# Score matmuls of a 16-head attention: from 128 partitions with masked keys to the head's own 32 partitions

## The reference

```python
q = (x @ Wq + bq).reshape(B, T, H, D).transpose(0, 2, 1, 3)      # B 4, T 1024, H 16, D 8
k = (x @ Wk + bk).reshape(B, T, H, D).transpose(0, 2, 1, 3)
v = (x @ Wv + bv).reshape(B, T, H, D).transpose(0, 2, 1, 3)
scores = jnp.einsum('bhqd,bhkd->bhqk', q, k) * D ** -0.5
scores = scores + slopes[None, :, None, None] * (i - j)          # first attention only
scores = jnp.where(causal, scores, -jnp.inf)                     # first attention only
out = jnp.einsum('bhqk,bhkd->bhqd', softmax(scores), v)
out = out.transpose(0, 2, 1, 3).reshape(B, T, C) @ Wo + bo
```

## Time and profile before

| what | value |
| --- | --- |
| median of 3 runs | 2288.22 us (2284.65 to 2291.63) |
| profiled execution, span | 2287.5 us |
| TensorE matmul busy | 2102.9 us, 92% |
| VectorE busy | 1671.8 us, 73% |
| ScalarE busy | 1373.5 us, 60% |
| POOL busy | 977.3 us, 43% |
| mean granted TensorE clock | 0.959 of full |
| at1 | from about 50 to 740 us |
| at2 | from about 803 to 1720 us |

### The profile page before, as it was taken

How to read it: one execution, slowest core, us unless ns; L and a number is a source line. 1 busy time by engine, 2 the same in 40 slices (tenths; PEclk the granted TensorE clock), 3 DMA queues, 4 the chain that set the end, 5 groups by cost and what they waited for, 6 DMA issues and landing times. The chain is left out here.

```text
span 2287.5 us, 41083 instructions
## 1 busy us (share of the span) xinstructions
PE 2102.9 (92%) x11100; PEld 1223.1 (53%) x11100; DVE 1671.8 (73%) x3157; ACT 1373.5 (60%) x2647; POOL 977.3 (43%) x744
## 2 busy tenths in 40 slices
PE   5899999999999679999999999999993999999996
PEld 4455555555554534555555555555531666666664
DVE  5766667666672787777777777778822899998986
ACT  4266566666666616666666666666672655555654
POOL 3665464553610355333333333342002466565554
PEclk7799999999999679999999999999996999999998
DMA  2000000000000300000000000000001100000000
GB/s 59 1 2 1 3 1 1 2 2 1 1 1 2 110 0 1 2 1 1 2 1 1 2 1 1 1 1 1 1 1 61 51 19 19 2 19 19 19 10 10
DMA packets 27508, 24.96 MB, mean 11 GB/s; under 512 B 2409, under 2 KB 21110, under 8 KB 27282
## 3 DMA queue, kind: packets, MB, share of 16 engines
q1 hardware_dynamic: 26400, 21.91, 3.2%
q10 hardware_dynamic: 882, 0.36, 0.1%
HBM read 13.87 MB, written 6.29 MB: 9 GB/s over the span
## 5 line engine op out<-in xcount | busy, mean ns | idle before, releaser
L466 DVE TENSOR_REDUCE at_mx<-at_a 128x1 f32<-128x512 f32 (+3 forms) x1632 | 1010.8, 675 | 358.7 <-PE at_a L333 249.5
L415 ACT ACTIVATE at_probs<-at_b 128x512 f32<-128x512 f32 (+3 forms) x1792 | 888.6, 558 | 474.0 <-PE at_b L360 292.7
L333 PE MATMUL at_a<-at_km,at_fq 128*128 128x512 f32 (+1 forms) x1632 | 704.8, 439 | 20.4 <-DVE at_mx L466 9.8
L360 PE MATMUL at_b<-at_fqm,at_km 128*128 128x512 f32 (+3 forms) x1792 | 710.8, 404 | 11.4 <-ACT at_probs L415 7.6
L333 PEld LDWEIGHTS at_a<-at_km,at_fq 128*128 128x128 f32 x1632 | 316.3, 194 | 290.0 <-DVE at_mx L466 224.4
L360 PEld LDWEIGHTS at_b<-at_fqm,at_km 128*128 128x128 f32 x1792 | 339.8, 191 | 205.5 <-ACT at_probs L415 120.3
L378 PE MATMUL at_pv<-at_probs,at_vst 128*32 128x512 f32 (+3 forms) x3584 | 437.9, 561 | 1.5 <-ACT at_probs L415 1.5
L556 POOL TENSOR_TENSOR at_hi<-at_u,split_sign 128x512 fp32r<-128x512 f32 x120 | 124.9, 1041 | 441.1 <-ACT at_u L404 306.5
L1172 ACT ACTIVATE t_hid<-t_bank_h,b1t 128x512 f32<-128x512 f32 x256 | 174.3, 689 | 195.9 <-DVE t_hid_lo L1306 113.1
L1306 DVE TENSOR_TENSOR t_hid_lo<-t_hid,t_hid_hi 128x512 fp32r<-128x512 f32 x256 | 225.6, 917 | 15.0 <-ACT t_hid_hi L1179 11.8
L569 POOL TENSOR_TENSOR at_km<-at_fk,head_mask 128x2048 fp32r<-128x2048 f32 x60 | 216.1, 3602 | 11.2 <-POOL at_fk L567 11.0
(11 more groups left out here) (211 smaller groups left out, 2410.3 us busy)
## 6 DMA issues: line engine op xcount, KB each, us to landing
t_raw<-L_ffn_W SPq DMA_DIRECT2D x16, 256.0 KB, 3.1
x_first<-L_attn_x SPq DMA_DIRECT2D x4, 512.0 KB, 7.3
second_x_in<-L_attn_x SPq DMA_DIRECT2D x8, 256.0 KB, 3.1
kept<-second_joined SPq DMA_DIRECT2D x8, 256.0 KB, 2.6
kept_u<-second_normed SPq DMA_DIRECT2D x8, 256.0 KB, 2.0
t_heads_in<-tokens SPq DMA_DIRECT2D x8, 256.0 KB, 2.6
t_u_in<-kept_u SPq DMA_DIRECT2D x8, 256.0 KB, 3.1
t_x_in<-kept SPq DMA_DIRECT2D x8, 256.0 KB, 3.1
```

Source lines behind the costliest of these rows:

```text
L333: mm = pe.matmul(scores, fq[g][:, qt * P:(qt + 1) * P], km[g][:, heads[0]:heads[0] + k, kh * HALF:kh * HALF + w], start=True, stop=not dia ...
L360: mm = pe.matmul(out[:, 0:w], km[g][:, j, kt * P:(kt + 1) * P], fqm[g % 2][:, q0:q0 + w], start=True, stop=not diagonal)
L415: act.activation(probs[(t % 2) * GH + j][:, 0:w], b_bank[n % 3][:, 0:w], ACT.Exp).then_inc(exp_done, 1)
L466: dve.tensor_reduce(mx[:, kh, qt, heads[0]:heads[0] + k], a_bank[n % 3][:, 0:k * w].rearrange("p (k w) -> p k w", k=k), AX.X, ALU.max).the ...
```

## The change

Keys are no longer copied per head. The split writes `fk` for a whole slot, as `fq` is, and `km` with its multiplication goes, on VectorE (first slot) and POOL. Each score matmul takes the 32 partitions of its head from both operands, so that head j lies at row group j. The mask matmuls L337 and L363 still contract 128 partitions. An `a` chunk holds one head, so at1 has 48 chunks in a slot where it had 38; at2 keeps 64. The `b` matmuls and Exps of a step go through the heads in the order 2, 3, 0, 1 (`b_head`). The step counts of the splits' semaphores follow.

```diff
--- before.py
+++ after.py
@@ -65,10 +65,8 @@
...
                     continue
-                per = max(1, HALF // n)
-                per = 4 if per >= 4 else per
-                for j in range(0, GH, per):
-                    self.chunks.append((qt, kh, list(range(j, j + per)), n))
+                for j in range(GH):
+                    self.chunks.append((qt, kh, j, n))
 
@@ -154,6 +152,12 @@
...
 
+def b_head(n):
+
+
+    return (n + 2) % GH
+
+
 class Register:
@@ -217,13 +221,12 @@
...
 
-        km = [sb(f"km{i}", [P, GH, T], F32R) for i in range(4)]
+        fk = [sb(f"fk{i}", [P, T], F32R) for i in range(4)]
         fq = [sb(f"fq{i}", [P, T], F32R) for i in range(4)]
...
         part = sb("part", [P, HALF])
-        fk = sb("fk", [P, HALF])
         probs = [sb(f"probs{i}", [P, HALF]) for i in range(8)]
@@ -317,7 +320,7 @@
...
                     elif what == "a":
-                        qt, kh, heads, w = plan.chunks[n]
+                        qt, kh, j, w = plan.chunks[n]
                         _, g = where(b0, g0, ds)
@@ -325,17 +328,14 @@
...
                         done(pe, a_read, NA, s - back, k)
-                        out = a_bank[n % 3]
+                        scores = a_bank[n % 3][:, 0:w]
                         diagonal = causal and kh * HALF + w == (qt + 1) * P
-
-                        k = len(heads)
-                        scores = out[:, 0:k * w].rearrange("p (k w) -> p k w", k=k)
-                        mm = pe.matmul(scores, fq[g][:, qt * P:(qt + 1) * P],
-                                       km[g][:, heads[0]:heads[0] + k, kh * HALF:kh * HALF + w],
+                        rows = slice(HW * j, HW * (j + 1))
+                        mm = pe.matmul(scores, fq[g][rows, qt * P:(qt + 1) * P],
+                                       fk[g][rows, kh * HALF:kh * HALF + w],
                                        start=True, stop=not diagonal)
                         if diagonal:
-                            mm = pe.matmul(scores[:, :, w - P:w], ident16[:, :],
-                                           causal_mask[:, None, :].broadcast_to([P, k, P]),
+                            mm = pe.matmul(scores[:, w - P:w], ident16[:, :], causal_mask[:, :],
                                            start=False, stop=True)
@@ -347,7 +347,7 @@
...
                         _, g = where(b0, g0, ds)
-                        t, j = n // GH, n % GH
+                        t, j = n // GH, b_head(n)
                         qh, kt = plan.quads[t]
@@ -357,8 +357,9 @@
...
                         out = b_bank[n % 3]
-                        mm = pe.matmul(out[:, 0:w], km[g][:, j, kt * P:(kt + 1) * P],
-                                       fqm[g % 2][:, q0:q0 + w], start=True, stop=not diagonal)
+                        rows = slice(HW * j, HW * (j + 1))
+                        mm = pe.matmul(out[:, 0:w], fk[g][rows, kt * P:(kt + 1) * P],
+                                       fqm[g % 2][rows, q0:q0 + w], start=True, stop=not diagonal)
                         if diagonal:
@@ -405,12 +406,12 @@
...
                     elif what == "b":
-                        t, j = n // GH, n % GH
+                        t, j = n // GH, b_head(n)
                         qh, kt = plan.quads[t]
...
                         done(act, b_made, NB, s, n)
-                        if j == 0:
+                        if n % GH == 0:
                             done(act, pv_done, NQ, s, t - 2)
@@ -436,7 +437,7 @@
...
                         un = u[n % 2]
-                        own = 5 * h if m else 5 * h + 3
+                        own = 4 * h + 2 * (n % 2)
                         done(dve, proj_read, 4, s, n)
@@ -445,26 +446,16 @@
...
                         dve.wait_ge(dve_step, own + 2)
-                        if m == 0:
-                            dve.tensor_tensor(fq[g][:, half], part[:, :], un[:, :],
-                                              ALU.add).then_inc(split_done, 1)
-                        else:
-                            dve.tensor_tensor(fk[:, :], part[:, :], un[:, :], ALU.add).then_inc(dve_step, 1)
-                            dve.wait_ge(dve_step, own + 3)
-                            dve.tensor_tensor(km[g][:, :, half],
-                                              fk[:, None, :].broadcast_to([P, GH, HALF]),
-                                              head_mask[:, :, None].broadcast_to([P, GH, HALF]),
-                                              ALU.mult).then_inc(split_done, 1)
+                        dst = fk if m else fq
+                        dve.tensor_tensor(dst[g][:, half], part[:, :], un[:, :], ALU.add).then_inc(split_done, 1)
                     elif what == "a":
-                        qt, kh, heads, w = plan.chunks[n]
+                        qt, kh, j, w = plan.chunks[n]
                         done(dve, a_made, NA, s, n)
...
                             done(dve, m_step, 2, s - 1, 0)
-                        k = len(heads)
-                        dve.tensor_reduce(mx[:, kh, qt, heads[0]:heads[0] + k],
-                                          a_bank[n % 3][:, 0:k * w].rearrange("p (k w) -> p k w", k=k),
+                        dve.tensor_reduce(mx[:, kh, qt, j:j + 1], a_bank[n % 3][:, 0:w],
                                           AX.X, ALU.max).then_inc(a_read, 1)
@@ -513,7 +504,7 @@
...
 
-            count = 2 * 3 + 2 * 2
+            count = 4 * 2
             pool.sem_inc(pool_step, count - 2 + count)
@@ -550,7 +541,7 @@
...
                     await_(split_done, 4, s, n - 1)
-                    step = 5 * h if m else 5 * h + 3
+                    step = 4 * h + 2 * (n % 2)
                     half = slice(h * HALF, (h + 1) * HALF)
@@ -560,16 +551,8 @@
...
                     await_(pool_step, count, s, step + 1)
-                    if m == 0:
-                        pool.tensor_tensor(fq[g][:, half], part[:, :], un[:, :],
-                                           ALU.add).then_inc(split_done, 1)
-                    else:
-                        pool.tensor_tensor(fk[:, :], part[:, :], un[:, :], ALU.add).then_inc(pool_step, 1)
-                        await_(pool_step, count, s, step + 2)
-                        pool.tensor_tensor(km[g][:, :, half],
-                                           fk[:, None, :].broadcast_to([P, GH, HALF]),
-                                           head_mask[:, :, None].broadcast_to([P, GH, HALF]),
-                                           ALU.mult).then_inc(split_done, 1)
+                    dst = fk if m else fq
+                    pool.tensor_tensor(dst[g][:, half], part[:, :], un[:, :], ALU.add).then_inc(split_done, 1)
```

## The result

The changed kernel takes 2978.33 us (median of 4 runs, 2976.74 to 2997.45) against 2286.83 us before: a ratio of 1.304 (95% interval 1.300 to 1.308). Predicted were 2813 us, with 2350 to 3300 as the range. The profiled execution has a span of 2975.0 us, 687.5 more than that of before.

A forecast was written before the change was run, and what follows sets the result against it. TensorE, never idle, was taken as the bound. 2287.5 + 530 (at1's 15 slots) + 20 (its last slot and opening) - 16 (at2) - 9 (km) = 2812.5, so 2813 us; range 2350 to 3300.

The forecast's parts named there:

- likeliest case: At1 partly at the low clock, three to nine tenths of it: 2650 to 3030 us, chance 0.48.
- step 5: TensorE's clock in at1: six tenths guessed at 1.2 GHz, where a slot takes 96 us; mean slot 76.0 us, +35.3.
- Step 1: At1's 128-row masks among 32-row scores: two switches, 0.30 us a pair, 64 pairs, +19.2 us a slot.
- Step 2: One head per at1 chunk: ten more weight loads of 0.11 us each, +1.2 us a slot.
- Step 3: Scores on different row groups overlap: -3.2 us a slot in at1, -1.0 us a slot in at2.
- the bank loop: At2's step waits on three score banks, a 1.39 us chain from first to fourth b; steps under 2.8 us mean misread.
- Step 4: The km products go: four VectorE products of 2.29 us before at1's and at2's first reductions, -9 us; POOL's nothing.
- Its own signs: Expected in traces: 0.65 us per 512-wide pair, at1 clock 0.6 to 0.8, b's 1.39 us, TensorE near 100%, VectorE half.
- Clock in at2: Rival: the clock falls in at2 as well as at1, at2 +202 us with half of it low; 3366 us, chance 0.16.
- The clock holds in at1: Rival: at1 stays at full clock and pays only switches, chunks and overlap; 2538 us, chance 0.22.
- hidden masks: Rival: at1's switch to the mask costs nothing, slot 38.7 us; 2230 us, faster than before, chance 0.08.
- Row tiles give what column tiles give: Rival: scores run at once, VectorE bounds at2 at 42 us a slot, -192 us; 2360 us, chance 0.04.

The follow-up runs named there:

- E4: Changed kernel with each mask matmul cut to its head's 32 rows, three quarters of the mask left out; 2442.32 us (one run).
- e3: Kernel before with only at1's masks cut to 32 rows, scores still at 128, most of the mask left out; 2710.27 us (one run).
- e12b: Kernel before with one zero-weight matmul of 32 rows and 128 columns added behind the second b of each at2 step; 2367.21 us, 1.033 of before.
- e5: Kernel before with one head in each at1 chunk, 48 chunks a slot in place of 38; 2308.49 us, 1.009 of before.
- e7: Changed kernel with all scores and masks on head 0's 32 rows, other heads and three quarters of the mask left out; 3075.51 us (one run).
- e2: Changed kernel with row groups and one head a chunk in at2 only, at1 as in the kernel before; 2327.44 us, 1.014 of before.
- e9: e2 plus one zero matmul of 128 rows and 512 columns in 13 of 16 steps of an at2 slot; 2277.96 us, 0.995 of before.
- e1: Changed kernel with the whole mask on each head's 32 rows, as four accumulating matmuls; 2588.64 us, 1.121 of before.
- e8: Changed kernel with two zero-weight matmuls of 128 rows and the score's width before each at1 mask; 3006.43 us (one run).
- e11: e7 with 64 rows in place of 32, heads 2 and 3 and half the mask left out; 2405.18 us (one run).

## Why the prediction was right or wrong

**Side and cause: right.** Slower; at1 carries the loss, as the masks' switches and the clock. E4 shows it: with the masks on the score's rows, 35 of the 42 us a slot are gone. The time lies in the likeliest case's own range (2650 to 3030), near its upper end. The five rows of the table add to 163 us above what the prediction summed: at1's slots 634 against 530, its edges 48.8 against 11 (20 less the 9 of km), at2's slots -17.6 against -15, and what follows them 22.4 against -1. That the time fits so well is in part luck: two large errors, in the share of the low clock and in the length of a slot at it, went opposite ways (step 5).

**Step 1, masks: right in kind, mis-sized.** 0.30 us a pair was taken, and 0.22 to 0.24 measured (the changed kernel, e3, e12b). 64 pairs are 15 us and not 19.2., nearest in form, gave 0.30, and the earlier trace rows the lower bound of 0.20; the truth lay between.

**Step 2, chunks: right.** 1.2 us a slot predicted (ten weight loads of 0.11 are 1.1), 42.2 - 41.0 = 1.2 in e5.

**Step 3, overlap: the bank loop sets the step, but it was misread in size, and the overlap in at1 was left out where it counts.** The loop measured 1.26 us from the first b to the fourth, against 1.39. "Overlap can only bring the first b closer to the first a, by 0.11" failed: they start together, which is worth the whole 0.33, and the step went to 2.67 and 2.79 us, not 2.94. The prediction's own sign for a misread loop, steps under 2.8 us, came true. At full clock an at2 slot is 1706.64 - 1654.69 = 52.0 us (L465), from 54.1; of the 16 x 0.3 = 5 us won by the steps, 2.1 remain. The projections take most of the rest. The last two slots of at2 have none, and there the slot went from 51.3 to 47.2 us (the last one, before and changed):

```profile
1623.55:1674.88 51.33, 51.24 (x276) 27.04 (x272) 42.53 (x74) 34.62 (x66) 0.40 (x1) 1.00 0.00 1
2292.86:2340.03 47.17, 39.72 (x276) 14.02 (x272) 42.47 (x75) 34.42 (x67) 0.40 (x1) 1.00 0.00 1
```

So the four projections of a slot cost 4.8 us in the changed kernel and 2.8 before, 2.0 more, where the prediction had 0.8 for all eight blocks of 128 rows. Whether their switches do this, or a wait in the bank loop behind them, no run separates. The lower clock takes the rest, down to the -1.1 that was measured over the fifteen slots, which by chance is near the predicted -1.0. In at1 at the low level an unmasked score can lie wholly beside a masked one; if all do, it is 32 x 0.43 = 14 us a slot, an estimate, where the term had 3.2.

**Step 4, km: right in sign, 6 us and not 9.** From VectorE's first split to the first reduction it is 52.13 to 64.53 us before and 52.53 to 62.14 changed in at1, 805.82 to 818.29 and 1483.43 to 1492.51 in at2: 2.8 and 3.4 us won, where the two products of each take 4.6. VectorE now waits 0.5 to 1.1 us for ScalarE's copy of each following projection block. In at1's opening this is hidden by what follows: from there to the first L474 it is 25.3 us before and 39.0 changed, the clock at 0.50 where it was 0.82.

**Step 5, the clock: the step that failed by most, in its share.** "Six tenths" of at1 at the low clock was a guess, and it was 0.96 (a mean of 0.52 between 0.50 and 1.00), outside even the three to nine tenths of the likeliest case. This was partly made up by the low slot, for which 96 us were predicted: the slots measured are 82.3 us at a mean of 0.54 and 85.0 at 0.52 (521.78 to 604.10 and 604.10 to 689.14 between two L465), so that one wholly at 0.50 would be some 87, an estimate from the two. At the predicted 96 us and 57.9, a share of 0.96 would have made the slot 93.5 us and the time some 3075. Rebuilt from single costs the low slot is 42 x 1.9 = 80, and 64 x 0.27 = 17, less 14 if every unmasked score hides, 83; the 4 us that are missing say that some of them do not. So of the 42.3 us by which the slot grew, 1.2 are the chunks, 15 the switches at full clock, and 26 the clock, net of the overlap. The reason given was only half of the matter: "about as thinly filled as the stretch that lost the clock" speaks of pairs and columns, and e7, as densely filled as before, lost its clock through its rows.

**Its own signs.** A 512-wide pair takes 0.58 us and not 0.65, the slot at the low clock some 87 and not 96, the b's 1.26 and not 1.39 from first to fourth, and at1's clock is 0.52, outside the 0.6 to 0.8 that was named. TensorE's records are near 100% busy in at1 (99%) and VectorE fell to 35% there, as named.

**Clock in at2: the rival was half right.** It fell, to 0.95, and in e2 to 0.89; this cost about half of what the overlap won in the changed kernel and all of it in e2, but not the 202 us of that rival. Behind the last L465, where no a is issued any more, it is 0.65 for 45 us where it was 1.00, and from there to the end 22 us are lost (in e9, with 1.00 there, one). A small share of the mechanism, then, but the one that decides e2.

**The other rivals.** "The clock holds in at1" (2538) fell with 0.52, and "hidden masks" (2230) with 0.23 us a pair. "Row tiles give what column tiles give" (2360) fell at its bound: tiles start together (the a and the b at 1706.55), but the banks, not VectorE, set the slot. The Trainium skill (TensorEngine Tiling (Array Packing), Key Properties) has a drain at each change of mode, and the traces agree as far as every such change costs time: 0.23 us for two. For four row tiles the Trainium skill (TensorE: Matmul & The Clock Gate, Measured speedup vs the span model) gives 3.07 times; here the step gained 0.3 of 3.05 us, as its matmuls wait for banks.

**Open.** How few rows, or how many switches, cost the clock how much: only 32, 64 and 128 rows were run, and neither cause was varied beyond that. Why the same 32 rows leave at1 at 0.53 and at2 at 0.74 (e7) no run separates; at1 has the masks and the narrower scores. What makes a projection dearer among row groups is open too.

## What to carry to other kernels

A matmul of 32 rows takes as long as one of 128 (0.23 us from score to score at full clock in both, e7), so row groups win only where scores of different groups may start together and their output banks are free; count the banks first. A mask in the stream that keeps another row count pays some 0.23 us for the way there and back, and the four projections of an at2 slot cost 2.0 us more than before: where it can be done, put such a matmul on the same row group, even as four matmuls (e1). And look at the granted clock of each stage after such a change: where it fell, a zero matmul of full rows in a wait that is there anyway can bring it back and win time (e9); one that the path has to carry brings the clock back too, but not the time (e8).

## What the runs showed of the hardware

- Rows count for the clock. Matmuls of 32 rows with TensorE 99% busy ran at a mean of 0.74 of full clock in at2 and 0.53 in at1, 64 rows at 0.97 and 0.93, and 128 at 1.00 and 0.99 (e7, e11, before).
- Matmuls of 128 rows with zero weights raise the clock: 0.52 to 0.80 (e8), 0.89 to 0.97 (e9).
- Two switches between 128 and 32 rows, fp32 scores and a bf16 mask: 0.22 to 0.24 us at full clock, 0.27 at the low one. It hardly follows the clock.
- 54 switch pairs in a slot of at1 bring the clock to 0.71 with all scores at 128 rows (e3); 16 pairs in a slot of at2 leave it at 0.99 (e12b).
